# Transposing the row maxima before they are split, a new place for several steps of the order, and queries and keys as three float32r products

## The reference

```python
x = x + attention(layernorm(x), w_qkv, w_out, b_out)          # 16 heads of width 8
x = x + experts(layernorm(x), router_w, router_b, w1, w3, w2) # 4 experts, top 2

def attention(x, w_qkv, w_out, b_out):
    q, k, v = heads(x @ w_qkv.T)
    a = (q @ k.T) * scale
    a = a - max(a, axis=-1)                  # the row maxima
    s = where(a >= 0, pos(a), 1.0 / (1.0 - a * (1.0 - 0.5 * a * (1.0 - a / 3.0))))
    return (s / sum(s)) @ v @ w_out.T + b_out

def experts(x, router_w, router_b, w1, w3, w2):
    p = softmax(x @ router_w + router_b)     # two of four kept, renormalised: the gates
    return sum_e gates[e] * ((silu(x @ w1[e]) * (x @ w3[e])) @ w2[e])
```

## Time and profile before

| | |
|---|---|
| median of 3 runs | 1149.4 us (1149.16 to 1149.68) |
| the profiled execution: device time | 1149.13 us |
| the profiled execution: span of the trace | 1147.4 us |
| TensorE busy (matmul) | 1111.0 us, 97% |
| VectorE busy | 1005.3 us, 88% |
| ScalarE busy | 1000.1 us, 87% |
| GpSimd busy | 709.5 us, 62% |
| granted TensorE clock, mean | 0.997 of full speed |

### The profile page before, as it was taken

The page is one execution under the profiler, slowest core; times in us unless marked ns, Lnnn a source line. Parts: engine busy times, 40 slices in busy tenths (PEclk is TensorE's granted clock), DMA queues, the critical chain, the costliest instruction groups (busy, mean ns, idle before and its releaser), DMA issues.

```text
span 1147.4 us, 29043 instructions
## 1 busy us (share of the span) xinstructions
PE 1111.0 (97%) x9848; PEld 932.9 (81%) x9848; DVE 1005.3 (88%) x1821; ACT 1000.1 (87%) x1034; POOL 709.5 (62%) x941
## 2 busy tenths in 40 slices
PE   6889999999999999999999999999999999999998
PEld 5758888888888888888888888888888888888888
DVE  4878999999999999999999999999999999999834
ACT  0799999998989999899999999999989999999982
POOL 5345755766666667666576666566766567666530
PEclk9999999999999999999999999999999999999999
DMA  4544333233432233433223333323343322334100
GB/s 119 175 132 125 115 92 97 87 119 120 125 103 87 88 106 114 125 114 99 89 84 119 120 125 104 90 88 102 115 125 114 100 88 83 120 121 122 30 6 10
DMA packets 129103, 117.49 MB, mean 102 GB/s; under 512 B 15492, under 2 KB 123684, under 8 KB 129060
## 3 DMA queue, kind: packets, MB, share of 16 engines
q1 hardware_dynamic: 126852, 113.78, 32.4%
q10 hardware_dynamic: 2208, 3.15, 0.9%
HBM read 94.70 MB, written 21.09 MB: 101 GB/s over the span
## 4 chain that ended last, share of the span: by engine, by line
PE 82%; DVE 8%; issue 3%; ACT 2%; DMA 2%; POOL 2%; ACTq 0%; DVEq 0%; SPq 0%; POOLq 0%
PE banks L1264 32%; PE banks L1537 19%; PE sc L1350 10%; PE banks L1282 5%; DVE mx L944 4%; PE sc L1520 3%; DVE mx_split L994 2%; PE misc L1589 1%; PE misc L1397 1%; PE misc L1415 1%; PE misc L1590 1%; ACT poly L717 1%; PE banks L1520 1%; PE misc L1375 1%; PE misc L1579 1%
## 5 line engine op out<-in xcount | busy, mean ns | idle before, releaser
L457 POOL TENSOR_TENSOR hid<-hid,gate_all 128x512 f32<-128x512 f32 x240 | 377.7, 1635 | 155.3 <-DMA gate_all<-gate_scratch 145.1
L859 DVE SCALAR_TENSOR_TENSOR poly<-w_sq,sc 128x1024 f32<-128x1024 f32 x252 | 303.4, 1214 | 33.7 <-ACT w_sq L613 33.5
L1264 PE MATMUL banks<-xn_hi,w_hi 128*128 128x256 f32 x976 | 292.9, 300 | 0.8 <-DVE logits L976 0.4
L1264 PE MATMUL banks<-xn_lo,w_hi 128*128 128x256 f32 x976 | 275.3, 282 | 0.0
L1264 PE MATMUL banks<-xn_hi,w_lo 128*128 128x256 f32 x976 | 274.2, 281 | 0.0
L613 ACT ACTIVATE w_sq<-sc 128x1024 f32<-128x1024 f32 x252 | 255.6, 1028 | 7.8 <-PE sc L1350 3.7
L717 ACT ACTIVATE poly<-poly,two 128x2048 f32<-128x2048 f32 x128 | 249.2, 1991 | 0.4
L1537 PE MATMUL banks<-w_sb,hid 128*128 128x128 f32 x1920 | 246.1, 281 | 0.4 <-POOL hid L457 0.4
L944 DVE TENSOR_REDUCE mx<-sc 128x4 f32<-128x1024 f32 x192 | 230.6, 1216 | 11.8 <-PE sc L1520 9.2
L1537 PEld LDWEIGHTS banks<-w_sb,hid 128*128 128x128 f32 x1920 | 223.4, 191 | 16.7 <-POOL hid L457 0.8
L722 ACT ACTIVATE poly<-poly 128x2048 f32<-128x2048 f32 x128 | 236.7, 1895 | 0.0
(11 more groups left out here) (179 smaller groups left out, 1346.6 us busy)
## 6 DMA issues: line engine op xcount, KB each, us to landing
qk_scratch<-qk_split SPq DMA_DIRECT2D x32, 512.0 KB, 3.1
k_tile<-qk_scratch SPq DMA_DIRECT2D x128, 128.0 KB, 2.6
q_pad<-qk_scratch SPq DMA_DIRECT2D x256, 64.0 KB
q_tile<-qk_scratch SPq DMA_DIRECT2D x124, 128.0 KB, 2.5
k_stack<-qk_scratch SPq DMA_DIRECT2D x124, 128.0 KB
gate_all<-gate_scratch SPq DMA_DIRECT2D x30, 512.0 KB, 4.4
x_in<-in_L_attn_x_dram SPq DMA_DIRECT2D x32, 128.0 KB, 2.1
x_res<-in_L_attn_x_dram SPq DMA_DIRECT2D x32, 128.0 KB, 2.2
```

What stands on the lines that cost most here:

```text
L457: nc.gpsimd.tensor_tensor(h, h, by_token.unsqueeze(1).to_broadcast([128, 2, C, 128]), ALU.mult).then_inc(gated, 1)
L859: nc.vector.scalar_tensor_tensor(poly[:, u, :], w_sq[:, u % 2, :], 3.0, distance_buf(n, u), ALU.add, ALU.mult).then_inc(poly_ok, 1)
L1264: last = nc.tensor.matmul(dst, lhs[a], rhs[b], start=(k == 0), stop=(k == len(terms) - 1))
```

## The change

1. The maxima are transposed as they are (float32, [128 x 16] per half of the tokens). The two parts are made behind the transposes, by two VectorE operations on [16 x 256] that read `misc`, and the parts go to `q_pad` in two DMAs of half the size.
2. Queries and keys of the settled steps become three float32r products each. GpSimd makes the parts of their operand (`xn_split`), and, once, those of the weights (`proj_hi`, `proj_lo`).
3. Orders of the settled steps. VectorE: the eight maxima, the statistics, `queries_T`, `experts_added` and the copy of queries and keys have other places; that copy now stands ahead of the logits. TensorE: `router_operand` ahead of `score(3)`, `queries_operand` ahead of the weighted values, `queries_and_keys` ahead of `router_logits`, the values behind `distance(1)`. ScalarE: the copy of the values ahead of `silu(1)`, the third logarithm behind the statistics.

```diff
-        mx_split = sb("mx_split", [128, C, 2, H], F32R)
-        m_split = sb("m_split", [2 * H, S])
+        m_split = sb("m_split", [H, 2, S], F32R)
...
SP, second_half:
+                    sp.wait_ge(mx_hi_ok, m_split_at)
+                    sp.dma_start(q_pad[par][MROW:MROW + 1, :, :, :].bitcast(F32),
+                                 m_split[:, 0, :].bitcast(F32)).then_inc(m_stacked[par], 16)
                     sp.wait_ge(m_ok, m_split_at)
-                    sp.dma_start(q_pad[par][MROW:MROW + 2, :, :, :].bitcast(F32), m_split[:]).then_inc(m_stacked[par], 16)
+                    sp.dma_start(q_pad[par][MROW + 1:MROW + 2, :, :, :].bitcast(F32),
+                                 m_split[:, 1, :].bitcast(F32)).then_inc(m_stacked[par], 16)
...
GpSimd, second_half, behind the parts of xn2_T and ahead of pool.wait_ge(compared, ...):
+                    if settled(no(i, off)) and has(i, off + 2):
+                        n = no(i, off)
+                        pool.wait_ge(xnT_ok, n + 3)
+                        after(pool, qk_full, n + 2)
+                        nc.gpsimd.tensor_tensor(xn_split[:, 0, :], xn_T[:], zero[:].to_broadcast([128, S]),
+                                                ALU.add).then_inc(xn_hi_ok, 1)
+                        pool.wait_ge(xn_hi_ok, n - 1)
+                        nc.gpsimd.tensor_tensor(xn_split[:, 1, :], xn_T[:], xn_split[:, 0, :].bitcast(F32),
+                                                ALU.subtract).then_inc(xn_lo_ok, 1)
...
ScalarE:
                 if settled(n):
+                    if has(i, off + 1):
+                        values_copied()
                     silu(1)
                     values_T_copied()
                     square(2)
-                    if has(i, off + 1):
-                        values_copied()
...
                     log_of(1)
-                    log_of(2)
                 (statistics)
                 if settled(n):
+                    log_of(2)
                     weights_of(0)
...
VectorE:
                 def maxima_out():
                     m = n + 1
                     dve.wait_ge(mT_full, m + 1)
-                    after(dve, m_stacked[off % 2], pair_count(i, off, 16))
-                    nc.vector.tensor_copy(m_split[:], misc[0:2 * H, 0:S]).then_inc(m_ok, 1)
+                    after(dve, m_stacked[off % 2], pair_count(i, off, 32))
+                    nc.vector.tensor_scalar(m_split[:, 0, :], misc[0:H, 0:S], 1.0, None, ALU.add).then_inc(mx_hi_ok, 1)
+                    dve.wait_ge(mx_hi_ok, m + 1)
+                    nc.vector.scalar_tensor_tensor(m_split[:, 1, :], misc[0:H, 0:S], 1.0, m_split[:, 0, :].bitcast(F32),
+                                                   ALU.add, ALU.subtract).then_inc(m_ok, 1)
...
                     attention_added(i, off)
-                    if has(i, off + 1):
-                        scores_max(1)
                     sums()
-                    if has(i, off + 1):
-                        scores_max(2)
                     means()
                     if has(i, off + 1):
-                        for u in range(3, U - 1):
+                        for u in range(1, U - 2):
                             scores_max(u)
                     router_T()
                     if has(i, off + 1):
-                        scores_max(U - 1)
-                        split_maxima()
-                    experts_added()
-                    if has(i, off + 1):
-                        maxima_out()
+                        scores_max(U - 2)
                     if has(i, off + 2):
                         queries_T()
+                    if has(i, off + 1):
+                        scores_max(U - 1)
+                        maxima_out()
+                    experts_added()
+                    if has(i, off + 2):
+                        queries_and_keys_copied()
                     biased_logits()
                     shifted_logits()
                     compare()
-                    if has(i, off + 2):
-                        queries_and_keys_copied()
...
TensorE:
                     distance(0)
+                    distance(1)
                     values()
-                    distance(1)
...
                 def maxima_T():
-                    pe.wait_ge(mx_ok, n + 2)
+                    pe.wait_ge(s_used, U * (n + 2))
...
+                    if settled(n) and has(i, off + 2):
+                        pe.wait_ge(xnT_ok, n + 3)
                     for c in range(C):
-                        last = nc.tensor.transpose(misc[0:2 * H, c * 128:(c + 1) * 128],
-                                                   mx_split[:, c].rearrange("p h r -> p (h r)").bitcast(F32), ident[:])
+                        last = nc.tensor.transpose(misc[0:H, c * 128:(c + 1) * 128], mx[:, c, :], ident[:])
...
                 def queries_and_keys():
...
+                    if settled(n):
...
+                        pe.wait_ge(xn_lo_ok, n - 1)
+                        for s in range(2):
+                            last = exact(dst[:, s * S:(s + 1) * S], (proj_hi[:, s, :], proj_lo[:, s, :]),
+                                         (xn_split[:, 0, :], xn_split[:, 1, :]))
+                        last.then_inc(qk_full, 1)
+                        return
...
                     down(1, 2)
+                    router_operand()
                     score(3)
                     down(1, 3)
-                    router_operand()
+                    if has(i, off + 2):
+                        queries_operand()
                     weighted_values(i, off, 0)
                     weighted_values(i, off, 1)
-                    if has(i, off + 2):
-                        queries_operand()
                     if has(i, off + 1):
                         maxima_T()
                     up_a_unit(i, off - 1, 0)
-                    router_logits()
                     if has(i, off + 2):
                         queries_and_keys()
+                    router_logits()
```

More of the change, by code:

```diff
@@ L81, in attention_then_experts_kernel @@
         xn_T = sb("xn_T", [128, S])
+        xn_split = sb("xn_split", [128, 2, S], F32R)
+        proj_hi = sb("proj_hi", [128, 2, D], F32R)
+        proj_lo = sb("proj_lo", [128, 2, D], F32R)
         qk = sb("qk", [128, 2 * S])
@@ L185, in attention_then_experts_kernel @@
         xnT_ok = sem("xnT_ok")
+        xn_hi_ok = sem("xn_hi_ok")
+        xn_lo_ok = sem("xn_lo_ok")
+        proj_split_ok = sem("proj_split_ok")
         qk_full = sem("qk_full")
@@ L197, in attention_then_experts_kernel @@
         mx_hi_ok = sem("mx_hi_ok")
-        mx_ok = sem("mx_ok")
         m_ok = sem("m_ok")
@@ L481, in first_half @@
                     low_weights(1, w3_lo, w3_hi)
+                    pool.wait_ge(proj_ok, 4)
+                    nc.gpsimd.tensor_tensor(proj_hi[:].rearrange("p s d -> p (s d)"),
+                                            proj_T[:, 0:2, :].rearrange("p s d -> p (s d)"),
+                                            zero[:].to_broadcast([128, 2 * D]), ALU.add).then_inc(proj_split_ok, 1)
+                    pool.wait_ge(proj_split_ok, 1)
+                    nc.gpsimd.tensor_tensor(proj_lo[:].rearrange("p s d -> p (s d)"),
+                                            proj_T[:, 0:2, :].rearrange("p s d -> p (s d)"),
+                                            proj_hi[:].rearrange("p s d -> p (s d)").bitcast(F32),
+                                            ALU.subtract).then_inc(proj_split_ok, 1)
                 if has(i, off - 2):
@@ L987, in shifted_logits @@
                                             ALU.subtract).then_inc(shift_ok, 1)
-                def split_maxima():
-                    m = n + 1
-                    rows = mx[:]
-                    dve.wait_ge(s_used, U * (m + 1))
-                    after(dve, mT_full, m)
-                    nc.vector.tensor_scalar(mx_split[:, :, 0, :], rows, 1.0, None, ALU.add).then_inc(mx_hi_ok, 1)
-                    dve.wait_ge(mx_hi_ok, m + 1)
-                    nc.vector.scalar_tensor_tensor(mx_split[:, :, 1, :], rows, 1.0,
-                                                   mx_split[:, :, 0, :].bitcast(F32), ALU.add,
-                                                   ALU.subtract).then_inc(mx_ok, 1)
                 def maxima_out():
@@ L1339, in distances @@
                     pe.wait_ge(stacked[par], pair_count(i, off, STACKED))
-                    pe.wait_ge(m_stacked[par], pair_count(i, off, 16))
+                    pe.wait_ge(m_stacked[par], pair_count(i, off, 32))
                     if isinstance(i, int) and 0 <= m < 2:
@@ L1588, in queries_and_keys @@
                     dst = qk_out_of(m)
+                    if settled(n):
+                        if isinstance(i, int) and n == 2:
+                            pe.wait_ge(proj_split_ok, 2)
+                        pe.wait_ge(xn_lo_ok, n - 1)
[4 more added lines that the diff above has]
+                        return
```

## The result

| | before | after |
|---|---|---|
| median of the runs | 1149.54 us (4 runs, 1149.16 to 1149.78) | 1168.22 us (4 runs, 1167.31 to 1168.57) |
| ratio to before | | 1.0162, 95% interval 1.0144 to 1.0179 |
| the profiled execution: time, span | 1149.13, 1147.4 us | 1168.15, 1166.4 us |
| granted TensorE clock, mean | 0.997 | 0.995 |

The changed kernel is 18.7 us slower. The forecast was 1173 us, slower.

What follows compares the result with a forecast made beforehand. TensorE was taken as the bound at 33.86 us a step, two cross-engine loops a third of a microsecond behind; late logits make both about 34.70, so 28 x 0.84 = 23.5 us more: 1173 us, range 1147 to 1185.

Steps and rivals of the forecast that it cites:

- Loop A: Way from `distance(2)` through maxima transposes, logits, gates, `hidden(0)` and `polynomial(0)` back to `distance(2)`: 33.53 us before, slack 0.33, 34.66 after.
- The copy ahead of the logits: VectorE copies queries and keys before the logits, waiting for their products: router's chain 1.13 us late; the part that decides.
- The sum: Loops at 34.66 and 34.69 us, taken as 34.70: 0.84 a step over 33.86, times 28 steps, 23.5 us.
- the tie of the two loops: Both cross-engine loops nearly equal after the change, so a little is lost where they alternate: 34.70 taken per step.
- The maxima: With the split gone from VectorE, TensorE's 0.34 us wait before the transposes goes; the parts are made serially behind them.
- Gains nothing at `m_ok`: Finished parts of the maxima come at 528.57, the same time as before the change.
- The products: Queries and keys as six float32r products instead of two float32 ones on TensorE: 0.24 to 0.34 us less a step.
- GpSimd's pair is hidden: GpSimd's two `xn_split` operations run from some 526.0 to 527.5, while GpSimd is otherwise idle until 530.16.
- TensorE did not stay the bound: Rival: TensorE stays the bound, 33.18 us a step, 1130 us; chance 0.15 including a part of its gain.
- GpSimd's pair did not block VectorE: Rival: GpSimd's new pair holds up VectorE's first new operation, a further 0.48 us a step, 1186 us; chance 0.06.
- The mask's second DMA: Lands by 531.75 at the latest against `distance(0)` at 531.7; TensorE has over 0.5 us to spare, so costs nothing.
- Loop B: Way through the gates, eight `gate_hidden` and the down product back to the maxima: slack 0.35 before, 34.69 us after.

Runs made afterwards that it cites:

- e9: Kernel before plus a VectorE memset of 576 columns right ahead of the logits in the steps that changed: 1150.0 us, ratio 1.0005.
- e8: Kernel before plus a VectorE memset of 1280 columns right ahead of the logits in the steps that changed: 1170.4 us, ratio 1.0177.
- e4: Kernel before with only queries and keys moved ahead of the router's logits on TensorE and their copy ahead of the logits on VectorE: 1186.9 us.
- e3: e2 with VectorE's copy of queries and keys moved behind the comparisons, the rest of the change kept: 1129.6 us, ratio 0.9828 of before.
- e2: Changed kernel with TensorE's router logits back ahead of queries and keys, and the experts' addition ahead of maxima_out on VectorE: 1168.6 us.
- e5: e3 with the maxima as before: split on VectorE, both parts transposed, one copy, one mask DMA: 1142.7 us, ratio 0.9936 of before.
- e11: Kernel before with maxima transposed as they are, parts made behind the transposes and two mask DMAs; products and orders of before: 1146.7 us.
- e6: e3 with queries and keys as two float32 products and without GpSimd's pair for them: 1135.4 us, ratio 0.9873 of before.
- e1: Changed kernel with only VectorE's copy of queries and keys moved back behind the comparisons: 1162.3 us, 1.011 of before.
- e10: e3 with the experts' addition behind maxima_out on VectorE, as in the changed kernel, instead of ahead of it: 1153.8 us, ratio 1.0041 of before.

## Why the prediction was right, step by step

**The bound of before.** TensorE, with two loops a third of a microsecond behind it. Loop A's slack was put at 0.33; the spare of 0.38 less the hand-over of 0.05 is 0.33. e9 and e8 show it from both sides.

**The copy ahead of the logits.** The step that was said to decide did: e4 shows it alone, e8 imitates it, and e3 takes it away (against e2, by moving nothing else). Its terms, as worked out and as the step above has them: transposes to first operation 0.53 and 0.53; first to second 0.45 and 0.44; second operation 0.42 and 0.41; hand-over 0.06 and 0.10; products to copy 1.01 and 0.99; copy to logits 0.60 and 0.61. Bounds of 0.18 and 0.66 had been kept for the two new operations; 0.41, the copy's, was right.

**The sum.** 34.66 was forecast for loop A; the step read has 34.69. The mean of 24 steps is 34.60: 25.22 + 3.02 + 4.51 + 0.59 + 1.21 + 0.05. The difference is in one link, the transposes to the first operation, which takes 0.42 or 0.53 in turns, 0.47 in the mean; the row read was one of 0.53. The 0.04 added for the tie of the two loops is hardly there: the way to the transposes is 25.22 in the mean, as forecast without it. That this term is right to 0.01 is luck. In e3, where `distance(2)` does not wait, the way takes 25.11; in the changed kernel `distance(2)` starts after a wait and takes 0.73 instead of 0.63 (509.97, as in e8), which puts the 0.10 back. The forecast had neither the shorter way nor the dearer start. So 0.73 a step, not 0.84, over the same 24 steps. The transposes of the trace before number 3 to 32 span 982.14 us (87.00 to 1069.14), after 1001.73 (86.60 to 1088.33), which is 19.6 more; what lies ahead of them and behind is 0.6 shorter, together the 19.0 of the spans. The first two and the last of the changed steps lose less than the others (0.54, 0.57 and 0.51 us), 0.6 us between them. So of the 4.5 us between 23.5 and 19.0, about 3.1 are the 0.11 a step (28 times), and 0.6 each the three unequal steps and the ends of the kernel.

**The maxima.** "Gains nothing at `m_ok`" held: the wait of 0.34 before the transposes went and one of 0.39 before the products came. e5 against e3 shows what the part is worth where TensorE is the bound: 13 us. e11 shows that it brings 2.4 without the orders that go with it.

**The products.** Worth 0.14 to 0.2 us a step where TensorE is the bound (e6), 0.24 to 0.34 forecast, so this term was put too high. In the changed kernel they also stand on loop A, where they are shorter than the float32 ones by 1.17 - 0.99 = 0.18 (e4 and after, products to copy, means of 24 steps; in both VectorE waits for them). GpSimd's pair is hidden: it ends at 535.38, and the products need it at 536.2.

**The rivals.** TensorE did not stay the bound: its waits before `up_b_unit(1)` and `distance(2)`, forecast at 0.6 and 0.3, are there. The rows mark 0.36 and 0.15 idle, counted from the end of the matmul before; counted from the place where the next start was due, 0.12 behind the start before (508.20 and 509.54), they are 0.52 and 0.31. GpSimd's pair did not block VectorE: the first new operation takes 0.41 in the step read, and it starts 0.37 after the pair's end, so it did not put that rival to the test. Another copy out of `misc` in the same trace did, `queries_T`, which VectorE runs while GpSimd is at work:

```profile
533.46 0.42 DVE L991 COPY xn_T<-misc 128x256 f32<-128x256 f32 x1
```

```profile
533.25 0.74 POOL L552 TENSOR_TENSOR xn_lo<-xn_T,xn_hi 128x256 fp32r<-128x256 f32 x1
```

It ends ahead of GpSimd's operation. Of its 31 runs 23 lie wholly inside one, and none takes more than 0.43, the most it took before too, where none did. So this copy, which reads `misc`, is not held as L994 is. L994 itself has one source, in SBUF, and was held. The sentence that the forecast quotes from the Trainium skill's "SBUF — State Buffer", Who interferes with whom, frees such an instruction outside the two-port modes; L994 agrees with it only if it ran in such a mode, which no run here shows.

The mask's second DMA did not hold up `distance(0)`; TensorE ran from 539.74 without an idle mark. Loop B was forecast to tie with loop A. It comes near and binds in a few steps only: the down product that needs the last of the gated values starts 0.19 us after they are done in the mean of 24 steps, 0.44 before, with 0.05 in the closest steps. The list of waits has, for the down products:

```profile
PEld banks L1550 <- POOL hid L465: 1.6, 5, 0.5
...
PE banks L1550 <- POOL hid L465: 0.7, 3, 0.3
```

Before, the same two lines were 0.8 us in 2 waits and 0.4 in 2.

**What stays open.** The first of the two operations of the maxima starts 0.42 or 0.53 us after the transposes, in turns, before as after; I did not look for the reason. And loop A itself holds a part that no kernel here shortened: the operation that makes the gates (L1049, 8 columns) takes 0.89 us beside GpSimd's `qk_split` (L481) and 0.17 in the 3 of 32 batches where it has none beside it; in the other 29 it ends 0.02 to 0.03 us after GpSimd's operation. What those 0.7 us are worth, in any of these kernels, was not tested.

## What to carry to other kernels

Before moving a step, ask in whose idle time it lies now: a copy of 0.69 us that filled a wait for another engine was free, and ahead of the logits it made them 1.5 us later (e2 against e3), in a chain with 0.33 of slack, since it waits there for products of TensorE. Write down each cross-engine loop with its slack, not the busy shares: VectorE lost 15 us of work and the kernel 19 us of time. A reordering is one change of several engines together: of the three moves that make e3 out of the changed kernel, one alone brings 6 us (e1), the two others together nothing (e2), another pair is still slower than before (e10), and all three bring 39 us.

## What the runs showed of the hardware that I had not expected

The same VectorE operation with both ends in SBUF (a constant added to 128 x 32 float32) takes 181 ns in the fill, 0.66 us in the kernel before and a median of 375 ns in e5, by how much of a GpSimd operation is left when it starts; beside one it ends 0.04 us after it, every time. The Trainium skill's "SBUF — State Buffer", Who interferes with whom, has VectorE's two-port modes and GpSimd exclude each other for a whole instruction; these three durations agree with that, though no run shows in which mode it ran. A copy out of PSUM beside a GpSimd operation is not held (0.43 us at most, in 23 cases). The two operations that replaced it read PSUM and take 0.41 us each on 16 partitions and 256 columns, as long as the copy of 32 partitions and 256 columns did. A pair of TensorE products that starts after a wait takes 0.10 us more than one that follows other products (0.73 and 0.63).
